# A fused attention and feed-forward layer on one core: the first K and Q rows turned by VectorE straight from PSUM, and a re-ordered lead of score maxima

## What is computed

```
Q, K, V = x Wq^T + bq, x Wk^T + bk, x Wv^T + bv      # 32 query heads, 8 key/value heads, head width 16
Q, K = rope(Q), rope(K)                              # q*cos + rot_half(q)*sin
w = softmax(Q K^T / 4);   attn = w V;   y = layernorm(x + attn Wo^T + bo)
g = (y gate^T)*gate_s;  u = (y up^T)*up_s            # inner width 1408
out = layernorm(y + ((silu(g)*u) down^T)*down_s)
```

## Time and profile before

| | |
|---|---|
| time, median of 3 runs | 1038.73 us (1037.86 to 1039.15) |
| the profiled execution: its own time | 1039.11 us |
| its span in the trace | 1037.2 us |
| PE busy | 1017.1 us, 98% of the span |
| DVE / ACT / POOL busy | 77% / 64% / 27% |
| first input product | 5.75 us after the span's start |
| first product of maxima step 0 | 27.82 us |
| first product of unit 0 | 62.53 us |

### The profile page before, as it was taken

How to read it: one execution, slowest core, us unless ns; L and a number is a source line. 1 busy time by engine, 2 the same in 40 slices (tenths; PEclk the granted TensorE clock), 3 DMA queues, 4 the chain that set the end, 5 groups by cost and what they waited for, 6 DMA issues and landing times.

```text
span 1037.2 us, 15698 instructions
## 1 busy us (share of the span) xinstructions
PE 1017.1 (98%) x5858; PEld 534.6 (52%) x5858; DVE 794.2 (77%) x1139; ACT 664.9 (64%) x1346; POOL 278.6 (27%) x287
## 2 busy tenths in 40 slices
PE   8999999999999999999999999999999999999996
PEld 3643344433444433443444433333348888888885
DVE  5899978899779799779898898899822566563535
ACT  2359977789778898779666687888872420222221
POOL 2742021152245532246310055444101001000002
PEclk9999999999999999999999999899999999999999
DMA  5273517233215522345140447431238311311011
GB/s 205 82 211 105 123 34 215 59 99 87 54 53 143 91 73 48 85 85 133 35 79 12 119 136 151 109 128 41 100 119 195 120 41 41 82 51 32 1 40 43
DMA packets 64433, 94.88 MB, mean 91 GB/s; under 512 B 37536, under 2 KB 37920, under 8 KB 62272
## 3 DMA queue, kind: packets, MB, share of 16 engines
q1 hardware_dynamic: 63776, 93.10, 34.4%
q10 hardware_dynamic: 576, 0.72, 0.2%
HBM read 53.95 MB, written 27.00 MB: 78 GB/s over the span
## 4 chain that ended last, share of the span: by engine, by line
PE 94%; DVE 3%; ACT 1%; DMA 1%; issue 0%; POOL 0%; SPq 0%; POOLq 0%; DVEq 0%
PE PS L470 29%; PE PV L489 24%; PE PSA L559 15%; PE PS L576 6%; PE PSA L448 5%; PE PS L387 4%; PE PS L515 2%; PE PSA L515 2%; PE PV L576 2%; PE PSA L387 1%; PE PS L429 1%; ACT Bn L784 1%; DVE nmx L991 1%; DVE nmx L987 1%; DMA mscr<-mrow 1%; DMA A<-in_wqk 0%
## 5 line engine op out<-in xcount | busy, mean ns | idle before, releaser
L784 ACT ACTIVATE Bn<-PS 128x512 f32<-128x512 f32 x1128 | 535.5, 559 | 97.9 <-PE PS L470 85.6
L448 PE MATMUL PSA<-Kt,Qt 48*128 48x512 f32 x1024 | 388.5, 461 | 1.2 <-DVE Kt L964 0.8
L470 PE MATMUL PS<-Qt,Kt 50*128 50x512 f32 x1128 | 385.8, 436 | 3.8 <-DMA Qt<-mscr 2.5
L987 DVE TENSOR_REDUCE nmx<-PSA 128x1 f32<-128x512 f32 x512 | 327.3, 679 | 39.7 <-PE PSA L448 39.7
L470 PEld LDWEIGHTS PS<-Qt,Kt 50*128 50x128 f32 x1128 | 183.4, 185 | 311.5 <-ACT Bn L784 284.3
L991 DVE TENSOR_REDUCE nmx<-PSA 128x1 f32<-128x1024 f32 x256 | 312.2, 1219 | 22.6 <-PE PSA L448 20.3
L489 PE MATMUL PV<-Bn 128*32 128x512 f32 x2048 | 274.6, 608 | 0.0
L448 PEld LDWEIGHTS PSA<-Kt,Qt 48*128 48x128 f32 x1024 | 176.3, 184 | 11.7 <-DVE nmx L987 3.3
L559 PE MATMUL PSA<-x1Th,wr 128*128 128x512 f32 x344 | 135.5, 394 | 0.0
L559 PE MATMUL PSA<-x1Tl,wr 128*128 128x512 f32 x344 | 134.5, 391 | 0.0
L820 ACT ACTIVATE sg<-PSA,gs 128x512 f32<-128x512 f32 x43 | 29.6, 690 | 128.1 <-PE PSA L559 128.1
(11 more groups left out here) (170 smaller groups left out, 909.4 us busy)
## 6 DMA issues: line engine op xcount, KB each, us to landing
Qt<-pscr SPq DMA_DIRECT2D x90, 128.0 KB, 5.2
A<-in_wf SPq DMA_DIRECT2D x11, 768.0 KB, 7.1
wr<-A SPq DMA_DIRECT2D x33, 256.0 KB, 2.8
pscr<-A SPq DMA_DIRECT2D x16, 512.0 KB, 3.5
vscr<-Bn SPq DMA_DIRECT2D x32, 256.0 KB, 3.0
Kt<-pscr SPq DMA_DIRECT2D x90, 64.0 KB, 2.8
A<-A SPq DMA_DIRECT2D x16, 256.0 KB, 3.7
Bn<-vscr SPq DMA_DIRECT2D x8, 512.0 KB
```

The source lines that it names most:

```text
L448: op = e.matmul(PSA[:, 2 * s + h, :], Qt[n % 3][p:p + NC_, g % 2, 128 * qt:128 * qt + 128], Kt[n % 3][p:p + NC_, 512 * h:512 * h + 512], s ...
L470: e.matmul(score_tile(i)[:, cols], Kt[n % 3][rows, 128 * kt:128 * kt + 128], Qt[n % 3][rows, g % 2, 512 * qh + cols.start:512 * qh + cols. ...
L784: e.activation(Pb[c % NP_][:, cols], score_tile(score_bank[c, p])[:, cols], ACT.Exp, scale=0.25).then_inc(*act_exp.next(piece(c, p)))
L987: e.tensor_reduce(col, slot_pair(s)[:, h, :], AX.X, ALU.max, negate=True).then_inc(*dve_max[s].next((k, 0) if h == 0 else k))
```

## The change

`turn_pairs` of quarters (0,0), (1,0) and (0,1) now reads the product from PSUM by itself: two operations on 64 partitions each add the bias, multiply with sin and write to the other half of the partitions (which is the swap), one on 128 partitions adds the bias and multiplies with cos, and one subtracts. ACT's `evacuate`, PE's `swap_pairs` and POOL's `cosines` of these quarters, the swap matrix and its load are gone; of quarter (1,1) the swap is now two copies on ACT. ACT and POOL begin the rounding of x (`round_x`, `low_x`) in the time that this leaves them. A second warm-up product (128 x 256) follows the first on PE. V rows 0 and 1 move ahead of maxima step 0.

In the lead there are three slots instead of two up to step 20 (the third is `PS2` banks 0 and 1), every step up to 23 is read by DVE in one instruction instead of half of them in two, and the first 16 maxima need no join. V rows, projections and selections are dealt out to the pairs of steps anew.

```diff
-        dve_max = counts_of("dve_max", range(2))
+        dve_max = counts_of("dve_max", range(3))
...
         def slot_of(k):
-            return (k + (k >= before_flag)) % 2
+
+            return k % 3 if k <= 20 else (k + (k >= before_flag)) % 2
 
         def by_halves(k):
 
-            return stream[k][2] < 2
+            return k >= 24 and stream[k][2] < 2
+
+        def last_steps(hh):
+
+            return sorted({slot_of(k): k for k in range(16 * hh, 16 * hh + 16)}.values())
+
+        def joined(hh):
+
+            return hh >= 1
...
+        def whole(hh):
+
+            if joined(hh):
+                return [dve_ms.at(("join", hh))]
+            return [dve_max[slot_of(k)].at(k) for k in last_steps(hh)]
+
         def slot_pair(s):
-            return PSA[:, 2 * s:2 * s + 2, :]
+            return PSA[:, 2 * s:2 * s + 2, :] if s < 2 else PS2[:, 0:2, :]
...
-            def swap_pairs(i, h, ps):
-                w.wait_ge(*act_ev.at(("first", i, h)))
-                w.wait_ge(*landed["swap"].at())
-                e.matmul(ps, swap, cols_of(i, h)[0], start=True, stop=True).then_inc(*pe_swap.next((i, h)))
...
+            e.matmul(PV[:, 0:256], Vflat[:, 0:128], Vflat[:, 0:256], start=True, stop=True)
             fill(0, 0, 0, 1, 2, 3)
-            fill(1, 0, 0, 1)
-            swap_pairs(0, 0, bank(0))
-            fill(1, 0, 2, 3)
-            fill(0, 1, 0, 1)
-            swap_pairs(1, 0, bank(2))
-            fill(0, 1, 2, 3)
+            fill(1, 0, 0, 1, 2, 3)
+            fill(0, 1, 0, 1, 2, 3)
+            fill(1, 1, 0)
             pick(0, 0, 0, PSA[:, 0, :], dve_lo.at((0, 0)))
-            fill(1, 1, 0)
-            swap_pairs(0, 1, bank(1))
+            fill(1, 1, 1, 2, 3)
             for a in range(2):
                 pick(1, 0, 2 + 2 * a, bank(2 * a), dve_lo.at((1, 0)))
-            fill(1, 1, 1, 2, 3)
             pick(0, 1, 0, PSA[:, 1, :], dve_lo.at((0, 1)))
-            bank_free[0:3] = [act_pick.at(("q", 0, 0)), dve_rope.at((0, 1)), dve_pick.at(("q", 0, 1))]
             first_rows = [[act_pick.at(("k", 1)), dve_pick.at(("k", 1)), act_pick.at(("q", 0, 0)), dve_pick.at(("q", 0, 1))],
                           [act_pick.at(("q", 1, 0)), act_pick.at(("q", 1, 1))]]
+            for t in range(2):
+                value_rows(0, t, 3)
             w.wait_ge(*act_pick.at(("k", 1)))
             w.wait_ge(*dve_pick.at(("k", 1)))
             w.wait_ge(*act_ev.at(("first", 1, 1)))
+            bank_free[2] = dve_pick.at(("q", 0, 1))
 
             halves = itertools.count()
 
@@ -662,31 +668,32 @@
                 for _ in range(times):
                     maxima_half(next(halves))
 
-            advance(4)
-            swap_pairs(1, 1, bank(3))
-            value_rows(0, 0, 0)
-            for k in range(7):
-                advance(4)
-                if k == 4:
-                    for a, i in ((0, 2), (1, 3)):
-                        pick(1, 1, 2 + 2 * a, bank(i), pool_cs.at("lo"))
-                        bank_free[i] = act_pick.at(("q", 1, a))
-                if k < 4:
-                    value_rows(0, 2 * k + 1, (2 * k + 1) // 4)
-                    if 2 * k + 2 < 8:
-                        value_rows(0, 2 * k + 2, (2 * k + 2) // 4)
-                else:
-                    h, k0 = divmod(2 * (k - 4), 4)
-                    project_half(0, h, (2, 3)[h], (k0, k0 + 1))
-            for k in range(LEAD):
+            def pick_last(a):
+                clear(bank_free[3])
+                pick(1, 1, 2 + 2 * a, bank(3), pool_cs.at("lo"))
+                bank_free[3] = act_pick.at(("q", 1, a))
+
+            for k in range(8 + LEAD):
                 advance(4)
                 if k == 0:
-                    project_half(0, 1, 3, (2, 3))
-                    project_half(1, 0, 0, (0,))
-                elif k == 1:
-                    project_half(1, 0, 0, (1, 2, 3))
+                    value_rows(0, 2, 3)
+                    value_rows(0, 3, 3)
+                elif k < 3:
+                    project_half(0, 0, 2, (2 * k - 2, 2 * k - 1))
+                elif k == 3:
+                    value_rows(0, 4, 2)
+                    pick_last(0)
+                elif k == 4:
+                    value_rows(0, 5, 2)
+                    value_rows(0, 6, 2)
+                elif k == 5:
+                    value_rows(0, 7, 2)
+                    pick_last(1)
                 else:
-                    project_half(1, 1, 3, ((0, 1), (2, 3))[k - 2])
+                    j, h = ((0, 1), (1, 0), (1, 1))[(k - 6) // 2]
+                    project_half(j, h, (2, 3)[h], (2 * (k % 2), 2 * (k % 2) + 1))
+            bank_free[0] = bank_free[1] = dve_max[2].at(20)
...
+            def evacuate_last():
+                raw, qrot, _, _ = cols_of(1, 1)
+                w.wait_ge(*pe_first.at((1, 1)))
                 w.wait_ge(*landed["bqk"].at())
-                m = (4, 0)[i]
-                e.activation(cols_of(i, h)[0], PSA[:, 2 * i + h, :], ACT.Identity, bias=bqk[:, m:m + 1]).then_inc(
-                    *act_ev.next(("first", i, h)))
+                e.activation(raw, PSA[:, 3, :], ACT.Identity, bias=bqk[:, 0:1]).then_inc(*act_ev.next(("first", 1, 1)))
+
+            def swap_last():
+                raw, qrot, _, _ = cols_of(1, 1)
+                w.wait_ge(*act_ev.at(("first", 1, 1)))
+                for p in (0, 64):
+                    e.copy(qrot[64 - p:128 - p, :], raw[p:p + 64, :]).then_inc(*act_ev.next("swapped"))
...
-            load(swap, sw_d, "swap")
             load(sel_in.rearrange("p (m c) -> p m c", m=6), sel_d, "sel")
-            evacuate(0, 0)
+            round_x(0, 1, 2, 3)
             w.wait_ge(*landed["sel"].at())
             e.copy(sel[:, :, :], sel_in.rearrange("p (m c) -> p m c", m=6)).then_inc(*act_pick.next("sel"))
+            round_x(4, 5, 6, 7)
             round_first(0, 0, dve_rope.at((0, 0)))
-            evacuate(1, 0)
-            evacuate(0, 1)
+            round_first(1, 0, dve_rope.at((1, 0)))
+            round_w(1)
             place(Kt[0][0:NC_, 0:512], PSA[0:NC_, 0, :], pe_pick.at((0, 0, 0)), ("k", 0))
-            round_first(1, 0, dve_rope.at((1, 0)))
+            place(Kt[0][64:64 + NC_, 0:512], PSA[64:64 + NC_, 0, :], pe_pick.at((0, 0, 0)), ("k", 0))
             round_first(0, 1, dve_rope.at((0, 1)))
+            evacuate_last()
             place(Qt[0][:, 0, 0:512], bank(0), pe_pick.at((1, 0, 2)), ("q", 0, 0))
-            evacuate(1, 1)
             place(Kt[0][0:NC_, 512:1024], PSA[0:NC_, 1, :], pe_pick.at((0, 1, 0)), ("k", 1))
-            round_w(1)
-            round_x(0, 1)
-            w.wait_ge(*pe_swap.at((1, 1)))
-            e.copy(cols_of(1, 1)[1], PV[:, :]).then_inc(*act_ev.next("swapped"))
+            swap_last()
+            round_w(2)
             round_first(1, 1, pool_cs.at("rope"))
-            round_x(2, 3, 4, 5, 6, 7)
-            round_w(2)
             round_w(3)
-            for a, i in ((0, 2), (1, 3)):
-                place(Qt[0][:, a, 512:1024], bank(i), pe_pick.at((1, 1, 2 + 2 * a)), ("q", 1, a))
-            for j in range(2):
-                for h in range(2):
-                    evacuate_raw(j, h, ((2, 3), (0, 3))[j][h])
+            evacuate_raw(0, 0, 2)
+            for a in range(2):
+                place(Qt[0][:, a, 512:1024], bank(3), pe_pick.at((1, 1, 2 + 2 * a)), ("q", 1, a))
+            evacuate_raw(0, 1, 3)
+            evacuate_raw(1, 0, 2)
+            evacuate_raw(1, 1, 3)
...
-            def turn_pairs(i, h, ps, rc):
-                raw, qrot, _, sin = cols_of(i, h)
-                w.wait_ge(*pe_swap.at((i, h)))
+            def turn_pairs(i, h):
+                raw, qrot, cos, sin = cols_of(i, h)
+                ps, m = PSA[:, 2 * i + h, :], (4, 0)[i]
+                w.wait_ge(*pe_first.at((i, h)))
+                w.wait_ge(*landed["bqk"].at())
                 w.wait_ge(*landed[f"sin{h}"].at())
-                e.tensor_tensor(qrot, ps, sin, ALU.mult).then_inc(*dve_rope.next(("swap", i, h)))
-                w.wait_ge(*dve_rope.at(("swap", i, h)))
-                w.wait_ge(*pool_cs.at((i, h)))
-                e.tensor_tensor(raw, rc, qrot, ALU.add).then_inc(*dve_rope.next((i, h)))
+                w.wait_ge(*landed[f"cos{h}"].at())
+                for p in (0, 64):
+                    e.scalar_tensor_tensor(out=qrot[64 - p:128 - p, :], in0=ps[p:p + 64, :], scalar=bqk[p:p + 64, m:m + 1],
+                                           in1=sin[p:p + 64, :], op0=ALU.add, op1=ALU.mult).then_inc(
+                        *dve_rope.next(("swap", i, h)))
+                e.scalar_tensor_tensor(out=raw, in0=ps, scalar=bqk[:, m:m + 1], in1=cos, op0=ALU.add, op1=ALU.mult).then_inc(
+                    *dve_rope.next(("cos", i, h)))
+                w.wait_ge(*dve_rope.at(("cos", i, h)))
+                e.tensor_tensor(raw, raw, qrot, ALU.subtract).then_inc(*dve_rope.next((i, h)))
...
-            turn_pairs(0, 0, bank(0), rcos[0])
+            turn_pairs(0, 0)
+            turn_pairs(1, 0)
```

(19 more changed lines are left out.)

35 lines of the change are left out of this document (16 added, 19 removed).

## The result

The changed kernel takes 1033.16 us in the median (1030.62 to 1033.18), the kernel before 1038.36 beside it on the same chip: a ratio of 0.994, 95% interval 0.9925 to 0.9954. A second set on another chip gave 1032.61 (1030.45 to 1034.81) and 0.9939 (0.9925 to 0.9953). One execution of the first set is left out: 1101.73 us, at a mean granted clock of 0.847. The forecast was 1032.5, between 1030.8 and 1035.2. By medians the change is worth 5.2 us in the first set and 6.2 in the second; 6.2 was forecast. The profiled execution took 1032.56 with a span of 1030.7.

A forecast was written before the change was run, and what follows sets the result against it. PE is busy for 98% of the span, with DVE setting the lead's pace, so time saved before unit 0 should stay saved. 3.1 + 3.5 - 0.4 = 6.2 us, giving 1032.5 us, range 1030.8 to 1035.2.

The forecast's parts named there:

- The front, 3.1: Work ahead of maxima step 0: DVE starts at 10.84, step 0 comes at 24.7 instead of 27.82, 3.1 us earlier.
- The rival without the earlier rate: Front: PE's full rate comes no earlier, so the front gives 2.0 us and the time is 1033.6; chance 0.22.
- the prediction's way to 7.0: Front: full rate comes 4.3 us after gapless PE work starts, as now, so at 7.0 us with the gap filled.
- The lead, 3.5: From step 0's products to unit 0: 31.2 us instead of 34.7, at DVE's pace of 1.17 per step.
- the tail: End of the lead: from the read of step 22 to unit 0 takes 2.15 us, as now.
- the wait that I had put behind the read of step 22: End of the lead: steps 21 and 23 share a slot and six products follow, within the 2.15 to unit 0.
- The rival in which DVE keeps running dry: Lead: PE's in-order stream leaves DVE its old waits, 3.0 us more, time 1035.5; chance 0.10.
- Given back, 0.4: Behind unit 0: ACT waits for POOL's rope of job 0 and PE for ACT, costing 0.4 us (0 to 0.8).
- the rival in which it falls over the whole lead: PE's clock falls at its waits at 20 to 22 us; over the whole lead 25 more, 1057; slower chance 0.03.
- The maxima through DRAM: Between transpose and unit 0: a write lasting 8.1 us makes unit 0 1.8 late, time 1034.3; chance 0.05.
- The stall: Near 645 us: costs 6.1 us, should move unchanged; gone 1026.4, one more 1038.6; chance of differing 0.05.
- The prediction's sign of being wrong: Unit 0 begins later than 58, or at 56 with the rest taking longer than the 974.7 us of now.

The follow-up runs named there:

- number 1: The changed kernel without the second warm-up product on PE; 1033.9 us, ratio 0.9958.
- number 5: The changed kernel with SP issuing the two copies of job 0 ahead of the write of the first maxima; 1031.47 us, ratio 0.9929.
- 9: The changed kernel with the sixth feed-forward weight load (768 KB) issued behind the maxima's write near 631 us; 1028.38 us, ratio 0.9897.
- 12: The changed kernel itself measured once more, with no edit; 1032.61 us, ratio 0.9939.

## Why the prediction was right

**The front, 3.1.** Measured 3.30 (step 0 at 24.52; 24.7 was said). Each link held: passes 0.43 apart from about 7, the cos table as the start of DVE (10.73; 10.84), the full price for 64 partitions (1.53 for two), a turn of 3.08 (3.0), the last rest at 21.9 (22.0). The rival without the earlier rate is out, since the rate came before 9.1 us in all eleven profiles with the gap filled (number 1 has it open: 9.88). But the prediction's way to 7.0, the 4.3 us that the rate takes now counted from the start of gapless work, is no rule: all eleven start at 2.71 and come out between 5.76 and 9.03. That the first profile fell on 6.97 was luck. In the second profile of the same program step 0 is at 25.12, 2.7 earlier than before, between the forecast's 3.1 and the rival's 2.0.

**The lead, 3.5.** Measured 4.17 (30.54; 31.2 was said). Up to the read of step 22 the sum was right by errors that cancel: 28.28 from the first read, 28.3 said. Whole reads follow each other 1.13 apart and not 1.17, an addition costs 0.6 and not 0.7, but DVE waited 1.1 behind the first read and not 0.6, so that its waits in all, 0.77 + 0.30 + 0.81 = 1.9, are over the 1.5 that I named. What was off is the tail: from that read to unit 0 it is 1.49 and not 2.15. That read waited 0.81 for its products, which PE issues behind a projection piece, together with those of step 23 (52.80); by then the read of step 21 had freed step 23's slot, and the wait that I had put behind the read of step 22 was over. The rival in which DVE keeps running dry is out: the row of DVE's waits has 2.6 us, the part of the first read's ahead of step 0 included, in place of 4.4.

**Given back, 0.4.** The mechanism is right and the size was not. POOL's rope ends 5.82 behind unit 0 (5.6 said) and ACT waits 0.56; the hand-over is 0.68 longer in one profile and up to 2.2 in others, because PE's 1.2 us of idle are sometimes followed by the half rate. I had priced waits there and left the clock to the rival in which it falls over the whole lead.

**The maxima through DRAM** took no part: unit 0 comes 9.06 behind the end of the transpose (9.2 said), at DVE's and PE's pace.

**The stall** moved as a block, 6.67 earlier, and cost 5.5 in both kernels (I had 6.1). But it isn't constant: 43.3 to 45.5 us over ten profiles with the load in its place. The span of the forecast, 1031.0, was 1030.7: 7.47 up to unit 0, less 0.68 in the hand-over, less 0.3 elsewhere. That it is met to 0.3 is in part luck: the second profile of the same program has a span of 1032.9, with the slower front, a hand-over 1.5 longer and a stall 0.4 longer. The prediction's sign of being wrong also asked that all behind unit 0 take no longer than the 974.7 of before; it took 975.6. That bound left out the 0.4 which the forecast itself gives back (1031.0 less 55.9 is 975.1); of the other 0.5, the hand-over has 0.3.

What stays open: what decides whether the clock falls in the hand-over. It fell in three of the nine profiles with three slots (numbers 5, 9, 12), twice behind a wait of 1.1 to 1.2 us, once with none, and not in six others, four of which have waits of 0.9 to 1.3 us. The same holds for the time at which the full rate comes at the start.

## What to carry to other kernels

Read a lead as a sum on the engine that sets its pace, and ask what a third buffer lets the other one do: here slot, dealing and form of the read belong together, and a whole read paid only with the third slot. When a gain at the front arrives short at the end, lay milestones through both profiles; the missing part stands between two of them, and so does what a lucky run lends to a worse kernel. An idle stretch of TensorE can cost more than its length: moving one large load from in front of a small write brought back 1.8 us of waiting and 3.0 beyond it, put down to the clock, and that was worth nearly as much as the whole change. And take a second profile of the same program before reading a microsecond out of the first: here the clock alone moved the front by 0.6 and the hand-over by 1.5.

## What the runs showed of the hardware

- The granted clock of the rows was 1.00 while passes ran 0.86 us apart ahead of 9.9 us (number 1); from 34 us on it tells both rates.
- With the gap ahead of the first input product filled, the full rate came at 5.76 to 9.03 us in eleven profiles, in two of one program at 6.97 and 9.03; with the gap open, at 9.88 and 10.04.
- DVE's operation with three inputs from PSUM takes 0.76 us for 64 partitions as for 128.
- A whole read of two banks lasts 1.22 us and the next begins 1.13 behind its start.
- A 16 KB write took 8.0 us with two loads of 768 KB and the rows of K and Q queued ahead of it, and 6.2 with one of the loads.
- The clock fell (to a mean of 0.57 over 4 us) also where PE's rows show no idle time, at 58 us in number 5.
